# Attention over the batch dimension: position-major rows, scores only in the diagonal blocks, no mask

## The reference, cut to what matters

```
def _L1_attn_ref(x, Wq, Wk):            # x: (32, 256, 256) = s, b, d
    q = jnp.einsum('sbd,ed->sbe', x, Wq)
    k = jnp.einsum('sbd,ed->sbe', x, Wk)
    scores = jnp.einsum('sbd,tbd->bst', q, k) / sqrt(256)
    align = jax.nn.softmax(jnp.tanh(scores), axis=2)
    return jnp.einsum('bst,tbd->sbd', align, x)
x = x + _L1_attn_ref(_layernorm(x), L1_attn_Wq, L1_attn_Wk)
```

## Time and profile before

| | us |
|---|---|
| median of 3 runs (lowest, highest) | 3235.22 (3232.56, 3238.36) |
| span of the profiled execution | 3234.4 |
| PE busy, share of the span | 3043.9, 94% |
| DVE busy, share | 2320.8, 72% |
| ACT busy, share | 1779.4, 55% |
| POOL busy, share | 1275.4, 39% |

### The profile page before, as it was taken

One profiled execution on the slowest core, in us unless ns is written; L12 is line 12 of the kernel. 1 busy time (PEld: TensorE's weight loads), 2 busy tenths in 40 slices (PEclk: granted clock), 3 DMA queues, 4 the chain that ended last, 5 costly groups with the idle time before them and its releaser, 6 DMA issues. The chain is left out here.

```text
span 3234.4 us, 57384 instructions
## 1 busy us (share of the span) xinstructions
PE 3043.9 (94%) x21110; PEld 2129.1 (66%) x21110; DVE 2320.8 (72%) x4824; ACT 1779.4 (55%) x3246; POOL 1275.4 (39%) x1927
## 2 busy tenths in 40 slices
PE   5899999999999998799999896899999999999998
PEld 3666766776676764466666563577777777777765
DVE  4789989889999886242111683788888788888876
ACT  5788888888888873111111332545555554555553
POOL 5466666666666652000000550233333333333331
PEclk8999999999999997899999997999999999999999
DMA  7877777778777772433333344443333344333330
GB/s 152 147 109 113 121 108 105 114 113 113 113 118 104 107 96 38 161 112 99 115 122 114 120 159 77 62 68 62 62 58 59 62 68 68 63 60 58 58 51 14
DMA packets 290984, 301.17 MB, mean 93 GB/s; under 512 B 35126, under 2 KB 278310, under 8 KB 290704
## 3 DMA queue, kind: packets, MB, share of 16 engines
q1 hardware_dynamic: 276304, 273.43, 48.4%
q0 software_dynamic: 6144, 15.68, 2.2%
q10 hardware_dynamic: 8256, 8.39, 0.8%
HBM read 95.53 MB, written 50.40 MB: 45 GB/s over the span
## 5 line engine op out<-in xcount | busy, mean ns | idle before, releaser
L536 DVE TENSOR_REDUCE xa_mx<-bank 128x2 f32<-128x512 f32 x1024 | 663.1, 686 | 228.7 <-PE bank L526 219.3
L640 ACT ACTIVATE xa_p<-bank 128x512 f32<-128x512 f32 x1024 | 565.6, 596 | 301.6 <-PE bank L630 300.9
L651 DVE SCALAR_TENSOR_TENSOR xa_p<-xa_p,bank 128x1024 f32<-128x1024 f32 x256 | 303.7, 1217 | 91.3 <-ACT xa_p L640 74.7
L663 PE MATMUL bank<-xa_p,xa_v 128*32 128x256 f32 x4096 | 278.7, 390 | 1.4 <-DVE xa_p L651 0.9
L2090 POOL DMA_INDIRECT sa_y<-expert_out,sa_s x64 | 67.9, 1060 | 518.2 <-DMA expert_out<-ex_y 474.6
L992 ACT ACTIVATE xa_p<-bank 128x384 f32<-128x384 f32 x512 | 229.9, 503 | 59.2 <-PE bank L980 32.1
L1001 POOL TENSOR_SCALAR_AFFINE_SELECT xa_p<-xa_p 128x256 f32<-128x256 f32 x512 | 208.1, 431 | 125.7 <-ACT xa_p L992 125.4
L1866 ACT ACTIVATE ex_h<-bank,ex_b 128x512 f32<-128x512 f32 x64 | 44.0, 687 | 362.3 <-PE bank L1855 362.3
L1885 PE MATMUL bank<-ex_w,ex_h 128*128 128x256 f32 x1024 | 224.7, 380 | 1.2 <-issue 0.9
L1855 PE MATMUL bank<-ex_xt,ex_w 128*128 128x512 f32 x512 | 224.0, 596 | 0.7 <-ACT ex_xt L1846 0.7
L526 PE MATMUL bank<-xa_ks,xa_qs 96*128 96x256 bf16 x1024 | 199.1, 278 | 22.6 <-DVE xa_p L651 10.7
(11 more groups left out here) (294 smaller groups left out, 6702.7 us busy)
## 6 DMA issues: line engine op xcount, KB each, us to landing
ex_w<-ra_parts SPq DMA_DIRECT2D x384, 128.0 KB, 4.6
xa_ks<-xa_pk SPq DMA_DIRECT2D x384, 128.0 KB, 5.5
ex_w<-in_L_ffn_W SPq DMA_DIRECT2D x32, 1024.0 KB, 7.1
xa_qs<-xa_pq SPq DMA_DIRECT2D x192, 128.0 KB, 4.8
ex_w<-xa_pq SPq DMA_DIRECT2D x192, 128.0 KB, 4.5
ra_x<-in_x SPq DMA_DIRECT2D x32, 256.0 KB, 7.3
xa_ctx<-in_ctx_t SPq DMA_DIRECT2D x64, 128.0 KB, 4.8
queue<-zeros ACTq DMA_DIRECT2D x4, 2048.0 KB, 12.8
```

The lines of the kernel that those rows point to most:

```text
L536: c.nc.vector.tensor_reduce(c.xa.row_max[:, :, n], halves(c.banks[2 + n % 2]), AX.X, ALU.max).then_inc(s.max_taken, 1)
L640: c.nc.scalar.activation(c.xa.p_beside[:, n // 2 % 4, :, n % 2, :], halves(c.banks[n % 2]), ACT.Exp, scale=SCALE).then_inc(s.exp, 1)
L651: c.nc.vector.scalar_tensor_tensor(out=p, in0=p, scalar=1.0, in1=c.banks[bank][:, :].unsqueeze(1).broadcast_to([P, TC, 2 * S]), op0=ALU.mi ...
L663: m = c.nc.tensor.matmul(bank[WIDE * quad:WIDE * quad + WIDE, at + q0:at + S], v[:, kc, 4 * g + quad, :], p(4 * g + quad, kc), start=(kc = ...
```

## The change

Rows are laid out position by position: the DRAM views become `t q b g d`, so partition 32q + b holds item b of quarter q, and each position is a block of 32 partitions. The scores are then needed only in four 32 x 32 blocks on the diagonal of each table. They are computed as column tiles: 4 groups x 2 halves x 4 quarters = 32 float32 matmuls with 32 columns of weights and 32 moving columns, each at a tile position of its own. tanh runs over 128 columns into a new tile; four exp instructions of 32 partitions x 128 elements write into the diagonal blocks of a weight tile whose rest was set to zero once, at the start of the phase. The mask, its constant and what made it are gone. The slots of every engine are set anew; SP's store of step t-7 now lies between the loads of t and t+1.

```diff
-    rows = d["x2"].rearrange("b (t q g) d -> t b q g d", g=G, q=Q)
-    slots, gates = (d[n].rearrange("(b t q g) -> t b q g", b=B, g=G, q=Q) for n in ("slots", "gates"))
+    rows = d["x2"].rearrange("b (t q g) d -> t q b g d", g=G, q=Q)
+    slots, gates = (d[n].rearrange("(b t q g) -> t q b g", b=B, g=G, q=Q) for n in ("slots", "gates"))
...
-            m = c.nc.tensor.matmul(c.banks[bank][:, g * P:(g + 1) * P], r.xn_t[par][:, k, g * P:(g + 1) * P],
-                                   r.q[par][:, k, g * P:(g + 1) * P], start=(k == 0), stop=(k == KC - 1))
+            for q in range(Q):
+                rows, at = slice(q * B, (q + 1) * B), slice(g * P + q * B, g * P + (q + 1) * B)
+                m = c.nc.tensor.matmul(c.banks[bank][rows, g * B:(g + 1) * B], r.xn_t[par][:, k, at], r.q[par][:, k, at],
+                                       start=(k == 0), stop=(k == KC - 1), tile_position=(0, q * B))
...
 def act_d_tanh(c, t):
     c.act.wait_ge(s.scored, t + 1)
-    c.act.wait_ge(s.summed, 4 * (t - 1))
-    c.nc.scalar.activation(flat_weight(c, t), c.banks[par][:, :], ACT.Tanh, scale=1.0 / math.sqrt(D)).then_inc(s.tanh, 1)
+    c.act.wait_ge(s.exp, t)
+    scores = c.banks[par][:, 0:G * B].rearrange("p (g n) -> p g n", g=G)
+    c.nc.scalar.activation(c.sa.tanh[:, :, :], scores, ACT.Tanh, scale=1.0 / math.sqrt(D)).then_inc(s.tanh, 1)
 def act_d_exp(c, t):
     c.act.wait_ge(s.tanh, t + 1)
-    c.nc.scalar.activation(flat_weight(c, t), flat_weight(c, t), ACT.Exp).then_inc(s.exp, 1)
+    c.act.wait_ge(s.summed, 4 * (t - 1))
+    for q in range(Q):
+        rows = slice(q * B, (q + 1) * B)
+        m = c.nc.scalar.activation(weight[rows, :, rows], c.sa.tanh[rows, :, :], ACT.Exp)
+    m.then_inc(s.exp, 1)
-def dve_d_mask(c, t):
-    c.nc.vector.tensor_tensor(r.weight[par][:, :, :], r.weight[par][:, :, :],
-                              r.same[:, :].unsqueeze(1).broadcast_to([P, G, P]), ALU.mult).then_inc(s.weight, 1)
...
+    for ring in range(2):
+        c.step(c.dve_made, nc.vector.memset(r.weight[ring][:, :, :], 0.0))
...
-ROUND_D = dict(pe=9, dve=8, act=6, pool=2, sp=2)
+ROUND_D = dict(pe=9, dve=7, act=6, pool=2, sp=2)
...       (PE slots: turn, project, score, sum)
-    (27, 28) (30, 31) (34,) (41, 42, 44, 47)
+    (5, 6) (8, 10) (13,) (20, 21, 25, 27)
...       (DVE slots: add, moments, normed, mask, out)
-    (17,) (18,) (21,) (31,) (35, 36, 38, 40)
+    (2,) (4,) (7,) none (22, 24, 26, 27)
...       (ACT slots: xn_t, project, tanh, exp)
-    (20, 21) (22, 23) (24,) (25,)
+    (3, 4) (5, 7) (8,) (12,)
...       (SP slots: load, out)
-    (0,) (9,)
+    (0,) (15,)
-    out_rows = d["x4"].rearrange("b (t q g) d -> t b q g d", g=G, q=Q)
+    out_rows = d["x4"].rearrange("b (t q g) d -> t q b g d", g=G, q=Q)
```

More of the change, by code:

```diff
@@ L1997, in setup_positions @@
     r.wq, r.wk, r.both = c.sb("sa_wq", [P, KC, D]), c.sb("sa_wk", [P, KC, D]), c.sb("sa_wqk", [P, KC, D])
-    r.same, r.pick = c.sb("sa_same", [P, P]), c.sb("sa_pick", [Q, P])
     s = r.s = Box()
     s.x_in = [c.sem(f"sa_x_in{i}") for i in range(4)]
-    s.picked, s.met, s.same = c.sem("sa_picked"), c.sem("sa_met"), c.sem("sa_same_made")
     s.joined, s.both = c.sem("sa_joined"), c.sem("sa_both")
[L2003 to L2008, removed]
 def sp_positions(c, d):
@@ L2020, in pe_positions @@
     s, r = c.sa.s, c.sa
[L2021 to L2024, removed]
     c.pe.wait_ge(c.loaded, 16 * c.loads)
@@ L2032, in act_positions @@
     s, r = c.sa.s, c.sa
-    c.act.wait_ge(s.met, 1)
-    c.nc.scalar.activation(r.same[:, :], c.banks[6][:, 0:P], ACT.Copy).then_inc(s.same, 1)
     c.act.wait_ge(s.joined, 1)
@@ L2040, in setup_d @@
     nc, r, s = c.nc, c.sa, c.sa.s
+    r.weight = c.ring("sa_p", 2, [P, G, P])
     r.y, r.x3 = c.ring("sa_y", 2, [P, G, D]), c.ring("sa_x3", 4, [P, G, D])
@@ L2044, in setup_d @@
     r.var, r.rstd = c.sb("sa_var", [P, G]), c.sb("sa_rstd", [P, G])
-    r.q, r.out, r.weight = c.ring("sa_q", 2, [P, KC, G * P]), c.ring("sa_out", 2, [P, G, D]), c.ring("sa_p", 2, [P, G, P])
+    r.q, r.out = c.ring("sa_q", 2, [P, KC, G * P]), c.ring("sa_out", 2, [P, G, D])
+    r.tanh = c.sb("sa_tanh", [P, G, B])
     n = STEPS_D
@@ L2052, in setup_d @@
     s.projected, s.q = c.sem("sa_proj", 2 * n), c.sem("sa_q", 2 * n)
-    s.scored, s.tanh, s.exp, s.weight = (c.sem("sa_" + name, n) for name in ("score", "tanh", "exp", "w"))
+    s.scored, s.tanh, s.exp = (c.sem("sa_" + name, n) for name in ("score", "tanh", "exp"))
     s.summed, s.rec, s.out, s.out_there = c.sem("sa_pv", 4 * n), c.sem("sa_rec", 4 * n), c.sem("sa_done", 4 * n), c.pair("sa_out_there", 16 * n // 2)
@@ L2056, in setup_d @@
         c.step(c.dve_made, nc.vector.memset(r.xn[ring][:, :, D:D + 1], 1.0))
+    for ring in range(2):
+        c.step(c.dve_made, nc.vector.memset(r.weight[ring][:, :, :], 0.0))
     c.dve.wait_ge(*c.all_of(c.dve_made))
-    c.dve.wait_ge(s.same, 1)
+    c.act.wait_ge(*c.all_of(c.dve_made))
     c.pe.wait_ge(s.both, 1)
@@ L2230, in act_d_tanh, with act_d_exp @@
     c.act.wait_ge(s.scored, t + 1)
-    c.act.wait_ge(s.summed, 4 * (t - 1))
-    c.nc.scalar.activation(flat_weight(c, t), c.banks[par][:, :], ACT.Tanh, scale=1.0 / math.sqrt(D)).then_inc(s.tanh, 1)
-def act_d_exp(c, t):
-    s = c.sa.s
-    c.act.wait_ge(s.tanh, t + 1)
-    c.nc.scalar.activation(flat_weight(c, t), flat_weight(c, t), ACT.Exp).then_inc(s.exp, 1)
-def dve_d_mask(c, t):
-    s, r, par = c.sa.s, c.sa, t % 2
-    c.dve.wait_ge(s.exp, t + 1)
-    c.nc.vector.tensor_tensor(r.weight[par][:, :, :], r.weight[par][:, :, :],
-                              r.same[:, :].unsqueeze(1).broadcast_to([P, G, P]), ALU.mult).then_inc(s.weight, 1)
+    c.act.wait_ge(s.exp, t)
+    scores = c.banks[par][:, 0:G * B].rearrange("p (g n) -> p g n", g=G)
+    c.nc.scalar.activation(c.sa.tanh[:, :, :], scores, ACT.Tanh, scale=1.0 / math.sqrt(D)).then_inc(s.tanh, 1)
+def act_d_exp(c, t):
+    s, weight = c.sa.s, c.sa.weight[t % 2]
+    c.act.wait_ge(s.tanh, t + 1)
+    c.act.wait_ge(s.summed, 4 * (t - 1))
+    for q in range(Q):
+        rows = slice(q * B, (q + 1) * B)
+        m = c.nc.scalar.activation(weight[rows, :, rows], c.sa.tanh[rows, :, :], ACT.Exp)
+    m.then_inc(s.exp, 1)
 def pe_d_sum(c, t, g):
     s, r, bank = c.sa.s, c.sa, 4 + g % 2
-    c.pe.wait_ge(s.weight, t + 1)
+    c.pe.wait_ge(s.exp, t + 1)
     c.pe.wait_ge(*c.bank_out[bank])
@@ L2279, in pe_phase_d @@
     pe_d_first_turn(c)
-    for n in range((STEPS_D - 1) * period + 48):
-        for b, k in due(n, period, (27, 28), STEPS_D, first=1):
+    for n in range((STEPS_D - 1) * period + 28):
+        for b, k in due(n, period, (5, 6), STEPS_D, first=1):
             pe_d_turn(c, b, k)
-        for b, k in due(n, period, (30, 31), STEPS_D):
+        for b, k in due(n, period, (8, 10), STEPS_D):
             pe_d_project(c, b, k)
-        for b, _ in due(n, period, (34,), STEPS_D):
+        for b, _ in due(n, period, (13,), STEPS_D):
             pe_d_score(c, b)
-        for b, k in due(n, period, (41, 42, 44, 47), STEPS_D):
+        for b, k in due(n, period, (20, 21, 25, 27), STEPS_D):
             pe_d_sum(c, b, k)
@@ L2293, in dve_phase_d @@
     period = ROUND_D["dve"]
-    for n in range((STEPS_D - 1) * period + 41):
-        for b, _ in due(n, period, (17,), STEPS_D, first=1):
+    for n in range((STEPS_D - 1) * period + 28):
+        for b, _ in due(n, period, (2,), STEPS_D, first=1):
             dve_d_add(c, b)
-        for b, _ in due(n, period, (18,), STEPS_D, first=1):
+        for b, _ in due(n, period, (4,), STEPS_D, first=1):
             dve_d_moments(c, b)
-        for b, _ in due(n, period, (21,), STEPS_D):
+        for b, _ in due(n, period, (7,), STEPS_D):
             dve_d_normed(c, b)
-        for b, _ in due(n, period, (31,), STEPS_D):
-            dve_d_mask(c, b)
-        for b, k in due(n, period, (35, 36, 38, 40), STEPS_D):
+        for b, k in due(n, period, (22, 24, 26, 27), STEPS_D):
             dve_d_out(c, b, k)
@@ L2308, in act_phase_d @@
     period = ROUND_D["act"]
-    for n in range((STEPS_D - 1) * period + 26):
-        for b, k in due(n, period, (20, 21), STEPS_D):
+    for n in range((STEPS_D - 1) * period + 13):
+        for b, k in due(n, period, (3, 4), STEPS_D):
             act_d_xn_t(c, b, k)
-        for b, k in due(n, period, (22, 23), STEPS_D):
+        for b, k in due(n, period, (5, 7), STEPS_D):
             act_d_project(c, b, k)
-        for b, _ in due(n, period, (24,), STEPS_D):
+        for b, _ in due(n, period, (8,), STEPS_D):
             act_d_tanh(c, b)
-        for b, _ in due(n, period, (25,), STEPS_D):
+        for b, _ in due(n, period, (12,), STEPS_D):
             act_d_exp(c, b)
@@ L2325, in pool_phase_d @@
     period = ROUND_D["pool"]
-    for n in range((STEPS_D - 1) * period + 6):
-        for b, _ in due(n, period, (2,), STEPS_D, first=2):
+    for n in range((STEPS_D - 1) * period + 5):
+        for b, _ in due(n, period, (1,), STEPS_D, first=2):
             pool_d_gather(c, d["expert_out"], b)
```

(8 more changed lines are left out.)

2 lines of the change are left out of this document (removed).

## The result

| | us |
|---|---|
| before, median of 4 (lowest, highest) | 3236.79 (3232.56, 3242.49) |
| after, median of 4 | 3275.14 (3272.35, 3275.59) |
| ratio after / before, 95% interval | 1.012 (1.0108 to 1.0132): 35 to 43 us slower |
| profiled execution of after; its span | 3272.35; 3270.6 |

The forecast was 3255, slower by 20. The direction and the mechanism came, the size came nearly twice as large.

The account below looks back on a forecast made before the run. Phase D, bound before by a PE and ACT loop of 8.76 us, becomes bound by four DMA engines at 12.2 a step: 3234.4 + 20.8 (D) - 0.5 (phase C) = 3254.7, median about 3255, range 3245 to 3284.

Parts of the forecast that it names:

- 4 engines carry x2 and x4: Phase D loads and stores: with 4 outermost, 4 DMA engines instead of 16 carry each transfer, 5.2 us instead of 1.3.
- scores: PE in phase D: 64 small records per step take 0.6 us, the first 0.1 more, against 2.03 before.
- four exps: ACT in phase D: exp as four instructions takes 0.8 to 1.1 us against 0.63, costing nothing unless over 1.5.
- compute step: Phase D without DMA: PE 7.4, DVE 7.5 or 7.6, POOL under 7, so a step of 7.6 us.
- rival A: Phase D transfers stay on 16 engines, dealt by partitions; D steps at 7.6 us, time 3214, faster; chance 0.13.
- first store issued: Start of phase D: the first store is issued at about 1827.5, as before.
- first store's issue to store 8's landing: Phase D: store 0 issued about 1827.5, loads 8 to 15 precede stores 1 to 8, store 8 landed at 1934.
- middle step: Middle of phase D: load, store, small loads and gathers on four engines take 12.2 us a step (11.7 to 14.5).
- store 8's landing to store 10's issue: Late phase D: step 10's output waits for store 8's landing at 1934; step 11's outputs come at 1942.
- issue of the last store to its landing: End of phase D: the last output ends at 1971 and its store lands at 1978.5, 5.2 transfer plus 2.1 fixed.
- B: Four engines, and phase D's small matmuls bound by number, 2.05 to 4.0 us a step: 3265 to 3280; chance 0.08.
- C: Four engines, SP's issue stuck behind full queues and gathers slowed, 14.5 to 18 a step: 3275 to 3303; chance 0.10.

Follow-up runs that it names:

- e1: After, with each x2 load and x4 store issued as four transfers of 32 partitions: 3213.8 us, ratio to before 0.9942.
- e12: After, with each x2 load and x4 store issued as two transfers of two quarters (64 partitions): 3386.3 us, one run.
- e5: After, with the DRAM views of before (b outermost) and row order unfit for the diagonal blocks, only its time of use: 3212.2 us, ratio to before 0.9934.
- e14: After, with x4 stores and x2 loads in four transfers each, except loads 0 to 3 left whole: 3210.3 us, ratio to before 0.992.
- e13: After, with scores as full 128 x 128 tables (16 records) and x2 loads 4 to 7 in four transfers each: ratio to before 1.0116, D 179.9 us.
- e7: After, with scores as full 128 x 128 tables (16 records) and tanh reading the diagonal blocks in four instructions: ratio to before 1.0131, D 186.3 us.
- e15: After, with loads 0 to 7 and the last store in four transfers each and three output tiles: 3251.9 us, ratio to before 1.0053.
- e11: After, with loads 4 to 7 and the last store in four transfers each and three output tiles: 3261.0 us, ratio to before 1.0075.
- e8: After, with three output tiles instead of two: 3262.2 us, ratio to before 1.0092.
- e9: After, with only the store of the last step in four transfers of 32 partitions: 3270.9 us, ratio to before 1.0108.
- e2: After, with only the x2 loads in four transfers of 32 partitions, stores whole: ratio to before 1.0009, D 149.9 us.
- e3: After, with only the x4 stores in four transfers of 32 partitions, loads whole: ratio to before 1.0046, D 157.0 us.

## Why the prediction was right in kind and short in size

Against rows, by its own steps (times of the profiled executions):

| step of the prediction | forecast | measured |
|---|---|---|
| 4 engines carry x2 and x4 | yes | yes (q1 at 22.8%; e1, e12) |
| scores | 0.6, +0.1 | 0.76 when not dry |
| four exps | 0.8 to 1.1 | 1.25, under the 1.5 allowed |
| compute step | 7.6 | 7.55 (e1) |
| gain without the 4-engine transfers (rival A) | 3214 | 3213.8 (e1), 3212.2 (e5) |
| first store issued | 1827.5 | 1834.9 (+7.4) |
| first store's issue to store 8's landing | 106.5 | 106.7 |
| middle step | 12.2 (11.7 to 14.5) | by the stores' issues 92.5 / 8 = 11.6, by their landings 11.95 |
| store 8's landing to store 10's issue | 1 (7 before step 11's 1942) | 8.3 (+7.3) |
| from there to the last output | 36 | 36.2 |
| issue of the last store to its landing | 7.5 | 10.0 (+2.5) |

The three excesses sum to 17.2 of the 17.75 us between 1978.5 and 1996.25. They are the steps that failed, as sizes of terms; the pace of the four engines isn't among them. That its row agrees to 0.2 us is partly luck. The semaphore records, as far as they are kept, have store 0 landed at 1845.89 and store 8 at 1941.52. So the first landing took 11.0 us from its issue where about 9 were forecast, the eight steps after it 95.6 where 98 were, and the two errors cancel.

- "The first store is issued at about 1827.5, also as before." It came at 1834.9. Loads 0 to 3 were called hidden, and rightly (e14). What load 4, issued at 1801.4, does to the small gathers on the same four engines wasn't asked, nor that after 4.6 us of idle PE the projections run in part at the slow clock (5.56 us instead of 3.70). e13 against e7 shows what this start is worth: 6.4 us of D. e15 against e11 gives 8.7, but there later dry bursts go as well.
- "The output of step 10 waits for that landing" was right (1941.6 is the forecast 1934 plus the late start). The step after it was wrong: the four outputs were taken to follow at once. In DVE's order the first output stands ahead of the next add and moments, and the other three need sums that PE has placed between the next projections, so 7.8 us pass between the first and the last. e8 took 9.9 us away.
- The last store was priced as if it ran alone and at 5.2 us. Store 14 was issued 5.4 us ahead of it on the same engines and ran slower than that, so the last one had to queue: its landing took 10.0 us, not 7.5. e9 took 5.8 us away.

With all three mended, e11's D is 169.5 us and e15's 160.8, where the forecast's was 1978.5 - 1813.9 = 164.6. That is no proof that the three are the whole: both kernels also put fewer loads on the four engines than the forecast had, and e11 still has dry bursts.

One slip in the working: q0's share on the four engines is 19.6% of 90 / 10.3 us, or 1.7 us a step by the earlier trace rows, not 1.9, and the upper end 14.3. Nothing hangs on it.

Of the rivals, A stated the time of the mended kernel. B's number of instructions as such costs nothing (0.76 us), but its fear came in another form, records that run dry. C's sign was there, SP stuck for 4.3 to 5.7 us at its third load issue in seven of eight steps, but the middle step it wanted (14.5 to 18) was not. The likely reason, which no run tests, is that the issue waits behind transfers that have to go first anyway. The x2 and x4 landings never got a time in the list of issues, as forecast from the row stack: their semaphores aren't raised by sixteen landings.

## What to carry to other kernels

Before changing the order of a DRAM view, look at the outermost dimension that the DMA carries: if it falls from 32 to 4, cut the transfer so that the large one is outermost again (e1: 3213.8 instead of 3275.1, same layout). A queue's busy share that sticks at k/16, whatever is waiting to go, points to k engines (22.8% for four, 12.6% for two here). When such a resource is the bound, price separately what shares it at the start, what compute is still to come between a late landing and the end of that step, and the backlog ahead of the last transfer: here these three were 17.2 us, against a forecast loss of 20.

## What the runs showed of the hardware

- 64 score records on four column tiles start within 0.57 us, 9 ns apart, or 38 ns for a round of four (15 intervals). The floor of about 25 ns from start to start (the Trainium skill, TensorE: Matmul & The Clock Gate, "Wait — 56ns, not 53.3ns?") doesn't hold for this burst over four tiles: even one float32 matmul, two records, comes every 18 ns. The records don't name their tile, so for a single tile no row shows anything.
- A 4 KB packet of q1 kept its engine busy for 0.16 us (one store over sixteen engines), 0.17 (the middle of after, four), 0.20 (the middle of before, sixteen) or 0.23 (after's last two stores, four). So the price of one quiet transfer is a floor, and the number of engines doesn't set the difference; what does stays open.
- SP stuck at the issue of the gates only where load and store both went over few engines (after up to 5.7 us, e12 up to 5.4; e2 and e3 at most 0.74 in D).
- PE may run dry in a burst of 64 small records while POOL issues indirect DMAs, in both runs of one program and not in another: up to 4.8 us instead of 0.57 from the first record to the last.
